# A mixture of experts behind eight attention layers on one core: the router's exponential, its row norm and its PSUM banks rearranged

## What is computed

```python
h = _layernorm(x, axis=-1) * (1 + cb) + sb
scores = softmax(h @ router_w)
topk_scores, topk_idx = top_k(scores, 2)
combine = zeros.at[n, topk_idx].add(topk_scores)
g, u = h @ gate_w[e], h @ up_w[e]
y = (silu(g) * u) @ down_w[e]
routed = sum_e y[e] * combine[:, e]
shared = silu(h @ shared_gate_w) * (h @ shared_up_w) @ shared_down_w
out = x + gb * (shared + routed)
```

## Time and profile before

| | |
|---|---|
| median of 3 runs | 534.76 us (534.60 to 535.27) |
| profiled execution, its own time | 535.02 us |
| its span, first to last instruction | 532.9 us |
| mean granted TensorE clock | 0.99 |
| busy: TensorE, VectorE, ACT, POOL | 508.9, 439.8, 407.5, 295.5 us |

### The profile page before, as it was taken

One profiled execution on the slowest core, in us unless ns is written; L12 is line 12 of the kernel. 1 busy time (PEld: TensorE's weight loads), 2 busy tenths in 40 slices (PEclk: granted clock), 3 DMA queues, 4 the chain that ended last, 5 costly groups with the idle time before them and its releaser, 6 DMA issues.

```text
span 532.9 us, 8252 instructions
## 1 busy us (share of the span) xinstructions
PE 508.9 (96%) x1994; PEld 311.6 (58%) x1994; DVE 439.8 (83%) x1639; ACT 407.5 (76%) x594; POOL 295.5 (55%) x322
## 2 busy tenths in 40 slices
PE   8889999999999999999999999999999978989896
PEld 6446555555565555555555555555555666767684
DVE  5888888988888898889888888988888785869753
ACT  3768888888888888888788888888888465575552
POOL 4445556555665556555665556655557554545452
PEclk8999999999999999999999999999999998999899
DMA  8200010000001000100010010001000000000000
GB/s 246 85 16 1 7 40 15 5 17 23 15 5 40 15 0 5 40 15 5 20 34 0 5 40 15 5 13 27 1 1 1 1 0 2 20 1 21 1 16 24
DMA packets 16055, 11.22 MB, mean 21 GB/s; under 512 B 8205, under 2 KB 13837, under 8 KB 16037
## 3 DMA queue, kind: packets, MB, share of 16 engines
q1 hardware_dynamic: 15316, 10.42, 7.2%
q10 hardware_dynamic: 720, 0.60, 0.4%
HBM read 9.96 MB, written 1.05 MB: 21 GB/s over the span
## 4 chain that ended last, share of the span: by engine, by line
PE 79%; DVE 11%; issue 3%; POOL 3%; ACT 2%; DMA 1%; ACTq 0%; DVEq 0%; POOLq 0%
PE bank L430 19%; PE bank L421 14%; PE bank L296 12%; PE bank L442 5%; PE bank L418 5%; PE bank L338 4%; PE bank L343 4%; PE bank L339 4%; PE bank L539 2%; PE bank L540 2%; PE bank L538 2%; PE bank L598 1%; DVE sc L1250 1%; PE bank L583 1%; PE bank L586 1%
## 5 line engine op out<-in xcount | busy, mean ns | idle before, releaser
L430 PE MATMUL bank<-hid,wf 128*128 128x512 f32 x256 | 120.2, 592 | 0.0
L867 POOL TENSOR_TENSOR rsD<-veD,c_half 128x4 f32<-128x4 f32 x32 | 38.0, 1186 | 103.1 <-DVE veD L970 103.1
L421 PE MATMUL bank<-x,wf 128*128 128x512 f32 x192 | 93.0, 593 | 0.0
L731 ACT ACTIVATE hid<-bank,vbf 128x512 f32<-128x512 f32 x128 | 77.6, 693 | 0.3 <-PE bank L421 0.3
L941 POOL TENSOR_TENSOR xs_lo<-sc,xs_hi 128x512 fp32r<-128x512 f32 x36 | 47.6, 1322 | 53.2 <-ACT xs_hi L835 53.2
L430 PEld LDWEIGHTS bank<-hid,wf 128*128 128x128 f32 x256 | 46.1, 190 | 46.6 <-issue 31.1
L421 PEld LDWEIGHTS bank<-x,wf 128*128 128x128 f32 x192 | 35.0, 189 | 33.3 <-issue 16.3
L1055 DVE TENSOR_SCALAR x<-bank,vln 128x256 f32<-128x256 f32 x64 | 31.9, 540 | 23.9 <-PE bank L296 23.9
L984 DVE TENSOR_SCALAR xhB<-bank,meanB,rsB 128x128 f32<-128x128 f32 x128 | 43.7, 404 | 8.8 <-POOL rsB L867 8.8
L984 DVE TENSOR_SCALAR xhD<-bank,meanD,rsD 128x128 f32<-128x128 f32 x128 | 43.8, 405 | 6.3 <-POOL rsD L867 2.1
L701 ACT ACTIVATE g<-bank,vbf 128x512 f32<-128x512 f32 x31 | 21.4, 689 | 35.6 <-PE bank L430 35.6
(11 more groups left out here) (162 smaller groups left out, 1200.5 us busy)
## 6 DMA issues: line engine op xcount, KB each, us to landing
wf<-in_w_f SPq DMA_DIRECT2D x16, 256.0 KB, 2.6
wu<-in_w_unit SPq DMA_DIRECT2D x10, 192.0 KB
wqkv<-in_w_qkv SPq DMA_DIRECT2D x7, 192.0 KB, 2.4
x<-in_x SPq DMA_DIRECT2D x4, 256.0 KB, 4.9
out<-ot SPq DMA_DIRECT2D x4, 256.0 KB, 2.2
wo<-in_w_o SPq DMA_DIRECT2D x8, 64.0 KB, 1.8
wmod<-in_w_mod ACTq DMA_DIRECT2D x1, 256.0 KB, 5.2
vln<-in_v_ln SPq DMA_DIRECT2D x16, 1.0 KB, 1.7
```

What stands on the lines that cost most here:

```text
L421: mm = nc.tensor.matmul(ps_ff[j][:], wf1[:, j * P:(j + 1) * P], x2[(c - 2) % CH][:], start=True, stop=True)
L430: mm = nc.tensor.matmul(ps_f0[:], wf2[:, j, :], hid[:, j, :], start=(j == 0), stop=(j == FJ - 1))
L731: nc.scalar.activation(hid[:, j, :], ps_ff[j][:], ACT.Gelu_apprx_tanh, bias=vbf1[:, j:j + 1]).then_inc(h_ready, 1)
L867: nc.gpsimd.tensor_tensor(rs[buf(k, n)][:], ve[buf(k, n)][:], c_half[:], ALU.pow).then_inc(rstd_ready[k], 1)
```

## The change

- The rows of chunks 1 to 3 are normalised by ACT (`norm_rows`, at u = 5), as rs * x + nbias; POOL computes nbias = -mean * rs (`norm_bias`), for which VectorE now writes the negated mean. VectorE's normalisation of chunk 0 stays.
- The exponential of chunks 1 to 3 is taken as Silu(x - 1) divided by Silu(1 - x), which is -exp(x - 1); the factor goes out in the softmax. VectorE takes the reciprocal and the product.
- The broadcast writes ps_v for odd units and ps_d for even ones (ps_d alone in chunk 1 up to u = 5).
- The transposes of the normalised rows and of the weights go to ps_q for chunks 1 to 3, a bank that the scaled rows, the scores and the result use too.
- `weights` comes ahead of `mixture_sum`, and `scaled` for chunks 2 and 3 moves from u = 1 to u = 7 of the chunk before.
- POOL splits the weights behind other units (`LATE_LOW`).

```diff
+        nbias = [sb(f"nbias{i}", [P, T]) for i in range(2)]
+        exn, ones = sb("exn", [P, T, E]), sb("ones", [P, 2])
+        def side_bank(c):
+            return ps_q if c else ps_v
+        def cast_bank(i):
+            c, u = divmod(i, U)
+            return ps_v if u % 2 and not (c == 1 and u < 6) else ps_d
...
             def zf_to_tm(c):
+                if c:
+                    pe.wait_ge(cst_ready, c)
...
             def norm_to_fm(c):
-                if c:
-                    pe.wait_ge(cst_ready, c)
-                if c == 2:
-                    pe.wait_ge(x_ready, NI + CH)
-                transposes(ps_v, xh["F"], to_fm["F"])
+                if c > 1:
+                    pe.wait_ge(ot_ready, c - 1)
+                transposes(side_bank(c), xh["F"], to_fm["F"])
...
             def last_to_tm():
                 pe.wait_ge(y2_ready, NI)
-                pe.wait_ge(hf_ready, 2)
-                pe.wait_ge(cst_ready, 2)
+                pe.wait_ge(sc_ready, E)
...
             def broadcast(i):
-                if routed(i):
-                    pe.wait_ge(sc_ready, routed(i))
+                if c == 1 and u == 7:
+                    pe.wait_ge(x_ready, NI + CH)
+                same = [j for j in range(i) if j % U >= SHARED and cast_bank(j) is cast_bank(i)]
+                if same:
+                    pe.wait_ge(sc_ready, routed(same[-1]) + 1)
...
             def result_to_tm(c):
+                pe.wait_ge(cst_ready, min(c + 2, CH))
...
+            def norm_rows(c):
+                q = buf("F", c)
+                act.wait_ge(nbias_ready, c)
+                act.wait_ge(to_fm["F"], c)
+                for j in range(T):
+                    nm = nc.scalar.activation(xh["F"][:, j, :], x0[:, c, j, :], ACT.Identity,
+                                              bias=nbias[c % 2][:, j:j + 1], scale=rs[q][:, j:j + 1])
+                nm.then_inc(normed["F"], 1)
...
             def exponentials(c):
                 act.wait_ge(lg_ready, c + 1)
-                nc.scalar.activation(ex[:], lg[:], ACT.Exp).then_inc(ex_ready, 1)
+                if c == 0:
+                    nc.scalar.activation(ex[:], lg[:], ACT.Exp).then_inc(ex_ready, 1)
+                else:
+                    nc.scalar.activation(ex[:], lg[:], ACT.Silu, bias=ones[:, 1:2])
+                    nc.scalar.activation(exn[:], lg[:], ACT.Silu, bias=ones[:, 0:1], scale=-1.0).then_inc(ex_ready, 1)
...
+                if u == 5 and n < CH:
+                    norm_rows(n)
                 if u == 6 and n < CH:
                     second_norm(n)
                     split_h_hi(n)
+                if u == 1:
+                    weights(c)
                 if u == 1 and c:
                     mixture_sum(c - 1)
-                if u == 1 and n < CH:
-                    scaled(n)
+                if i == 1:
+                    scaled(1)
+                if u == 7 and c + 2 < CH:
+                    scaled(c + 2)
                 if u == 8 and n < CH:
                     exponentials(n)
-                if u == 1:
-                    weights(c)
...
+            LATE_LOW = {0: 6, 1: 7, 4: 8, 6: 9}
+            def norm_bias(n):
+                q = buf("F", n)
+                pool.wait_ge(agg_done["F"], 3 * n + 3)
+                pool.wait_ge(rstd_ready["F"], n + 1)
+                nc.gpsimd.tensor_tensor(nbias[n % 2][:], mean[q][:], rs[q][:], ALU.mult).then_inc(nbias_ready, 1)
...
                     if u == 4:
                         rstd("F", n)
+                        norm_bias(n)
...
-                if k + 6 < U:
-                    split_weights_lo(ORDER[k + 6:k + 7])
+                if k in LATE_LOW:
+                    split_weights_lo(ORDER[LATE_LOW[k]:LATE_LOW[k] + 1])
...
             def route_ranks(c):
                 step(n + 5, nc.vector.tensor_reduce(rank[:], v4(cmp_all), AX_X, ALU.add))
                 dve.wait_ge(ex_ready, c + 1)
+                if c:
+                    step(n + 6, nc.vector.reciprocal(exn[:], exn[:]))
+                    step(n + 7, nc.vector.tensor_tensor(ex[:], ex[:], exn[:], ALU.mult))
...
-                    if u == 5:
-                        second_norm(n)
...
-                    nc.vector.tensor_tensor(sc[i % 3][:], ps_d[:], su[i % 2][:], ALU.mult).then_inc(sc_ready, 1)
+                    nc.vector.tensor_tensor(sc[i % 3][:], cast_bank(i)[:], su[i % 2][:], ALU.mult).then_inc(sc_ready, 1)
```

More of the change, by code:

```diff
@@ L685, in _ @@
             first_norm(0)
[L686 removed]
+            act.wait_ge(consts_set, 6)
             def last_norm(c, d):
@@ L763, in second_norm @@
                     b = c * HB + h
-                    ev = nc.scalar.activation(half(hf[c], h), half(ps_v, h), ACT.Identity,
+                    ev = nc.scalar.activation(half(hf[c], h), half(side_bank(c), h), ACT.Identity,
                                               bias=mod[:, 3, b:b + 1], scale=m1[:, 1, b:b + 1])
                 ev.then_inc(hf_ready, 1)
+            def norm_rows(c):
[6 more added lines that the diff above has]
+                nm.then_inc(normed["F"], 1)
             def scaled(c):
@@ L793, in weights @@
                     act.wait_ge(bc_mm, (c - 1) * E)
-                nc.scalar.activation(cst[c % 2][0:2 * E, :], ps_v[0:2 * E, :], ACT.Copy).then_inc(cst_ready, 1)
+                nc.scalar.activation(cst[c % 2][0:2 * E, :], side_bank(c)[0:2 * E, :], ACT.Copy).then_inc(cst_ready, 1)
             def split_h_hi(n):
@@ L862, in _ @@
             nc.gpsimd.memset(c_tiny[:], 1e-30).then_inc(consts_set, 1)
-            pool.wait_ge(consts_set, 4)
+            for i in range(2):
+                nc.gpsimd.memset(ones[:, i:i + 1], 1.0 - 2 * i).then_inc(consts_set, 1)
+            pool.wait_ge(consts_set, 6)
             def rstd(k, n):
@@ L971, in variance @@
                                                op0=ALU.mult, op1=ALU.add).then_inc(var_ready[k], 1)
-                nc.vector.scalar_tensor_tensor(out=mean[q][:], in0=dif[q][:], scalar=-0.5, in1=s_even[:, :, 0],
-                                               op0=ALU.mult, op1=ALU.add).then_inc(agg_done[k], 1)
+                if k == "F" and n:
+                    nc.vector.scalar_tensor_tensor(out=mean[q][:], in0=dif[q][:], scalar=0.5, in1=s_even[:, :, 0],
+                                                   op0=ALU.mult, op1=ALU.subtract).then_inc(agg_done[k], 1)
+                else:
+                    nc.vector.scalar_tensor_tensor(out=mean[q][:], in0=dif[q][:], scalar=-0.5, in1=s_even[:, :, 0],
+                                                   op0=ALU.mult, op1=ALU.add).then_inc(agg_done[k], 1)
             def stats(k, n, src, eps):
@@ L1135, in _, with first_step @@
             STEPS = 9
+            def first_step(c):
+                return STEPS * c + 2 * max(c - 1, 0)
             def step(n, op):
@@ L1178, in route_ranks @@
             def route_ranks(c):
[L1179 removed]
+                n = first_step(c)
                 step(n + 5, nc.vector.tensor_reduce(rank[:], v4(cmp_all), AX_X, ALU.add))
                 dve.wait_ge(ex_ready, c + 1)
[L1182 removed]
+                if c:
+                    step(n + 6, nc.vector.reciprocal(exn[:], exn[:]))
+                    step(n + 7, nc.vector.tensor_tensor(ex[:], ex[:], exn[:], ALU.mult))
+                step(n + 6 + 2 * bool(c), nc.vector.tensor_reduce(sm[:], ex[:], AX_X, ALU.add))
                 nc.vector.reciprocal(rsm[:], sm[:])
[L1184 removed]
+                step(n + 7 + 2 * bool(c), nc.vector.scalar_tensor_tensor(out=comb[:], in0=rank[:], scalar=1.5, in1=ex[:],
                                                            op0=ALU.is_lt, op1=ALU.mult))
             def route_weights(c):
[L1188 to L1189 removed]
+                n = first_step(c)
+                step(n + 8 + 2 * bool(c), nc.vector.tensor_tensor(comb2[:], comb[:], rsm[:].unsqueeze(2).to_broadcast([P, T, E]),
                                                     ALU.mult))
```

18 lines of the change are left out of this document (6 added, 12 removed).

## The result

| | before | changed |
|---|---|---|
| median of 4 runs each, in turn on one chip | 535.01 us (534.60 to 535.41) | 531.53 us (531.39 to 531.66) |
| profiled execution, its own time | 535.02 us | 531.66 us |
| its span | 532.9 us | 529.4 us |
| mean granted TensorE clock | 0.990 | 0.996 |
| busy: TensorE, VectorE, ACT, POOL | 508.9, 439.8, 407.5, 295.5 us | 507.2, 438.2, 404.5, 295.1 us |

The ratio is 0.9950 with an interval of 0.9928 to 0.9971: faster by about 0.5%. The forecast was 533.0 us in a range of 528.6 to 535.2. The two sets of the changed kernel don't overlap (531.39 to 531.66 and 531.94 to 533.70 us); why is open.

The account below looks back on a forecast made before the run. TensorE's few large stands, with two stretches at 1.2 GHz behind them, were taken to bound the mixture. Chunks 0 to 2 gave 3.25 - 1.76 + 0.3 = 1.8 us: a median of 533.0 us, range 528.6 to 535.2.

Parts of the forecast that it names:

- chain: From the end of unit 8's weighted product to the matmul behind its down product: 6.6 us, 7.3 with chunk 0's later split.
- chunk 0's sum: Unit 8's product ends at 437.1, plus 7.3 is 444.4 against 447.61: 3.25 us won, the clock's 1.5 in it.
- The new product: VectorE's 128x32 product behind the reciprocal meets POOL's low half (0.75 to 2.05 after unit 8's product), done at 2.25 us.
- Chunk 1: Unit 18's product ends at 471.84, plus 6.6 is 478.44 against 476.42: 2.0 us lost, less 0.24.
- the 0.24: Wait for the weights' copy, between 476.42 and unit 22's broadcast at 478.77, which would go: 0.24 us set against chunk 1's loss.
- The rival of no meeting: VectorE and POOL miss each other and TensorE runs through: 6.5 us won, 528.3 us; chance 0.17.
- the rival of one meeting: Reciprocal under 0.39 us, new product ahead of POOL, only the masking waits: 3.9 us won, 530.9 us; chance 0.2.
- Rows on ACT: Four activations of 1.5 us: 1.2 won at chunk 0's transposes, 0.45 lost in chunk 1, 0.4 won in chunk 2.
- and that stays: VectorE's time from unit 7's weighted product to the start of unit 8's, comparisons between: 4.68 us, taken as unchanged.
- the term of chunk 2: Unit 28's product ends at 499.77, plus 6.6 is 506.4 against 506.71: 0.3 us won, its clock spell included.
- Reciprocal: VectorE's 128x32 reciprocal ahead of the new product: 0.51 us by the slope of 12 ns an element, lower bound 0.21.
- the second wait: POOL's split of 1.02 us behind unit 8's low half makes the masking wait again, to 3.45; the chain becomes 7.3.

Follow-up runs that it names:

- no_product: The changed kernel without VectorE's reciprocal and product, so its weights are not those of the reference: 529.09 us, 0.9895 of the kernel before.
- exp_back: The changed kernel with the exponential and its table loads back on ACT, without reciprocal and product: 529.19 us, 0.9899 of the kernel before.
- shared_bank_alone: The kernel before with only the shared bank for the transposes of normalised rows and weights in chunks 1 to 3: 534.61 us, 0.9994.
- norm_act_alone: The kernel before with only the rows normalised on ACT and the bias product on POOL: 529.52 us, 0.9913.
- second profiled execution: Profile from the changed kernel run once more with no edit; the execution took 531.94 us, the median of that set 533.15 us, 0.9975.
- one_bank: The changed kernel with all spread weights broadcast into ps_d again: 532.30 us, 0.9947 of the kernel before.
- late_ranks: The changed kernel with ranks, reciprocal, product, sums and masking moved from u = 9 to the next u = 0: 531.03 us, 0.9931.
- norm_and_bank: The kernel before with the rows normalised on ACT and the shared bank for the transposes: 527.65 us, 0.9875.
- awake_alone: The kernel before with eight idle transposes ahead of the broadcasts of units 9, 19 and 29: 532.95 us, 0.9966.

## Why the prediction was right, and where it was not

**Direction and chain: right, chunk 0's sum partly by luck.** The new product met POOL's low half, in two chunks of three in the first profiled execution and in all three in the second. The steps of chunk 0 against the forecast: transposes of the normalised rows 426.29 (426.2), end of unit 8's weighted product 437.49 (437.1), unit 9's first product 3.06 us after it (about 3.5 with the split), last layer's transposes 444.38 (444.4). The last agrees because two misses cancel. Unit 8's product ends 0.4 us late, since unit 7's came 1.3 us earlier and not 1.6, and the comparisons took 4.89 instead of 4.68; the chain from there is 6.89 instead of 7.3. Chunk 1 lost 1.66 us, where 2.0 was forecast: the 0.24 that I set against it lies behind 476.42, so it belongs to the third stretch (0.25 measured). ACT's rows cost chunk 1 the 0.4 us that I had given. The rival of no meeting was what no_product and exp_back show when the product is taken out: 529.1 and 529.2 us (528.3). The first median, 531.53 us, is in fact nearer to the rival of one meeting (530.9) than to the forecast of 533.0, though only chunk 2 went that way; the second, 533.15, is at the forecast.

**Rows on ACT, their own price: nearly right.** ACT's four activations took 1.65 us (1.5), POOL's bias 0.20 (0.2). The Trainium skill (ScalarE: Activation LUTs, What ACT_TABLE_LOAD costs) had given an estimate of 1.64, and the trace agrees with it.

**Rows on ACT, what they bring: the step that failed.** I took the relief as 1.2 us where the transposes waited, plus 0.4 of a broadcast, and wrote of the 4.68 us between the weighted products of units 7 and 8 "and that stays". It does not. What these microseconds are depends on how far behind POOL's low half of the rows the comparisons start. Over the profiled executions of the kernels before, changed, shared_bank_alone and norm_act_alone, 0.15 us behind it gives 4.89, 0.35 to 0.37 gives 4.68 to 4.72, 0.77 gives 4.16, and 1.12 to 1.19 gives 3.92 to 3.96. With the rows on ACT the distance is 1.13 in all chunks of norm_act_alone and 1.12 in chunks 1 and 2 of the changed kernel: one whole meeting instead of two. (shared_bank_alone gets there in chunks 1 and 2 with the rows on VectorE, but by a stand that costs more.) This shrinks the stands behind, and the stretches at 1.2 GHz that followed them are gone. Alone this part is worth 4.9 us as a median. In the change this shows as the term of chunk 2: 0.3 forecast, 1.89 measured. Of these, 1.32 us are unit 28's product ending earlier against the start of the stretch (497.25 - 474.85 = 22.40 instead of 500.14 - 476.42 = 23.72), 0.77 of it by the comparisons and about 0.3 by the copy of the weights, and 0.57 the chain behind it (6.00 instead of 6.57). The chain is that short only because the new product escaped POOL there. In the second profiled execution it did not, and this term is 1.46.

**Reciprocal: mis-sized.** 0.35 us for 0.51. By the slope of two small sizes I had overrated the price per element. My bound for the case of one meeting, 0.39, left out the 0.03 us between two instructions; with it the bound is 0.36, and 0.35 lies on it. The rank sum ends 0.33 us after unit 8's product and the reciprocal at 0.72, so that the new product starts at 0.75, just when POOL's low half does. So neither the forecast nor the rival holds for all chunks: met in 0 and 1, escaped in 2 and free to start with the sum and the masking. The masking then met POOL in chunks 0 and 2 and missed it in chunk 1. Whether the product meets POOL is decided within 0.01 us, so that it mostly did, as forecast with 0.51, is luck.

**Weights split later: a cost not seen.** I had counted the second wait behind unit 8's low half. In chunk 0 the split at 431.14 also pushes POOL's queue together in front of the comparisons (1.42 and 1.51 us), and the 3.92 us become 4.89: 0.97 lost in chunk 0. No run has this part alone, but the kernels that have it agree: with the rows on ACT and the split there, chunk 0 takes 4.89 to 4.93 us (changed, one_bank, no_product, exp_back, late_ranks), and 3.92 where the split is as before (norm_act_alone, norm_and_bank). norm_and_bank, which has neither this nor the second bank, is 1.5 us below exp_back, but their intervals overlap.

**Second bank, table loads, shared bank: right.** one_bank (532.30) and exp_back against no_product (0.1 us apart) show that the first two carry nothing, and the last layer's transposes wait no longer.

**Clock.** The stretches of 0.92 and 0.94 became 1.00 in the first profile, as I had left them in the sum with 1.5 us for chunk 0; in the second profile one came back and cost nothing. The prediction's 1.5 us for a stretch is what awake_alone measures (1.57 and 1.56). Within the kernel before time goes with them: 532.29 us at a mean clock of 1.0, 534.2 to 535.4 at 0.989 or 0.99. Together they are most of the changed kernel's gain in the profiled execution, 3.1 of 3.46 us; the forecast had them in its terms of chunks 0 and 2, and without them it says 1.3 us lost, where 0.3 was won.

**The sum.** 3.25 - 1.76 + 0.3 = 1.8 was forecast, 3.23 - 1.66 + 1.89 = 3.46 measured. (437.1 + 7.3 is 444.4, which gives 3.21 and not 3.25.) With the 0.24 where it belongs the forecast is 3.25 - 2.0 + 0.54: chunk 2 has 1.35 of the miss and chunk 1 the other 0.34.

Two parts of the change are good, and the second needs the first: 534.4 to 534.7 us with neither, 529.5 with the rows on ACT, 534.6 with the shared bank, 527.65 with both. The rest of the change gives 3.9 us of this back (5.5 by the second set), most of it by the exponential from Silus.

## What to carry to other kernels

Price a relief of one engine not by its length alone, but by which meetings with another engine's operations it moves or removes, and by the stands that end with them: 1.2 us of wait was worth 4.9 as a median. In the profiled execution it was 5.9, 2.8 of them by waits and meetings and 3.1 by two stretches at 1.2 GHz that were gone. Before a gain is put down to the work, look whether such a stretch has left the profile: here a kernel with the old order and eight idle transposes at three places reached the changed kernel's mark within 0.4 us. A bank that is shared moves a wait to the reader that used it last, so ask where that reader stands in its queue; only when VectorE's normalisation ahead of it was gone did sharing pay. Taking table loads from an engine that waits anyhow wins nothing, and what replaces them on an engine whose chain bounds costs more than its length: 3.5 us for 1.6.

## What was not expected of the hardware

- A VectorE product of two SBUF inputs takes 0.19 us or 1.32 us when it starts in the same hundredth of a microsecond as POOL's operation (498.00 and 438.24). The Trainium skill (SBUF — State Buffer, SBUF: two separate sides) tells of such exclusion between the two engines, in which the one that starts first keeps the other out for its whole instruction. The trace agrees on the wait, and a start 0.01 us behind POOL's (497.88 and 497.87) was held; where both start at the same time, no row tells who was first.
- While POOL runs three operations without a gap, VectorE's comparisons get through one by one, each stretched from about 0.42 to 1.42 and 1.51 us.
- A wait of 2.25 us at 490.05 is followed by a stretch at 1.2 GHz (shared_bank_alone), one of 2.28 us at 443.95 is not (norm_act_alone). Executions of one unchanged kernel spread by 3 us (the kernel before, 532.3 to 535.4 over all sets), with mean granted clocks of 0.989 to 1.0.
- The reciprocal of 128x32 took 0.35 us, four activations of 128 elements with two pointers 1.65 us.
